# Feed-forward entry of a four-layer block: last probability transposes inside attending, sums of x before variances, later transposes of x

## What is computed

```
x = x + tanh(g_xattn[0]) * xattn0(layernorm(x), ctx, ctx)        # one head, 154 keys
x = x + tanh(g_ffn[0])   * ffn0(layernorm(x))                    # 8 experts, every token
x = x + tanh(g_xattn[1]) * xattn1(layernorm(x), ctx, mask)       # 8 heads of 64
x = x + tanh(g_ffn[1])   * ffn1(layernorm(x))                    # routed to one of 8 experts

ffn0: for each expert: acc += (silu(x @ Wg) * (x @ Wu)) @ Wd     # 256 -> 1024 -> 256
```

## Time and profile before

| what | value |
|---|---|
| runs | 1256.52, 1256.78 and 1260.38 us, median 1256.78 |
| the profiled execution's own time | 1260.54 us, of which the span from first to last instruction is 1258.8 us |
| PE busy | 1232.6 us (98% of the span) |
| DVE busy | 1054.3 us (84%) |
| ACT busy | 729.2 us (58%) |
| POOL busy | 880.5 us (70%) |
| mean granted clock | 0.995 |

### The profile page before, as it was taken

One profiled execution on the slowest core, in us unless ns is written; L12 is line 12 of the kernel. 1 busy time (PEld: TensorE's weight loads), 2 busy tenths in 40 slices (PEclk: granted clock), 3 DMA queues, 4 the chain that ended last, 5 costly groups with the idle time before them and its releaser, 6 DMA issues.

```text
span 1258.8 us, 18431 instructions
## 1 busy us (share of the span) xinstructions
PE 1232.6 (98%) x6152; PEld 995.4 (79%) x6152; DVE 1054.3 (84%) x1775; ACT 729.2 (58%) x1509; POOL 880.5 (70%) x833
## 2 busy tenths in 40 slices
PE   7999999999999999999999999999999999999998
PEld 5778888888888888888888888888888887787775
DVE  5887889898899999999999999888999974667546
ACT  2455566656666666666666666666566545545543
POOL 3735688888887888888877888888888626443435
PEclk9999999999999999999999999999999999999999
DMA  4020200000110000000000000000100330000131
GB/s 137 26 92 1 94 26 26 26 26 26 41 36 26 26 26 26 26 26 26 26 26 26 26 26 26 26 26 31 42 29 1 117 118 1 18 26 10 35 98 63
DMA packets 42366, 48.28 MB, mean 38 GB/s; under 512 B 4239, under 2 KB 40143, under 8 KB 42015
## 3 DMA queue, kind: packets, MB, share of 16 engines
q1 hardware_dynamic: 38720, 43.07, 10.4%
q0 software_dynamic: 1440, 3.41, 0.8%
q10 hardware_dynamic: 2111, 0.63, 0.2%
HBM read 37.36 MB, written 10.29 MB: 38 GB/s over the span
## 4 chain that ended last, share of the span: by engine, by line
PE 91%; DVE 4%; ACT 3%; issue 1%; DMA 0%; POOLq 0%; ACTq 0%; POOL 0%; DVEq 0%
PE bank L1307 25%; PE bank L1308 25%; PE bank L1309 25%; ACT PC L1050 2%; PE bank L1545 2%; PE bank L1554 1%; PE bank L1269 1%; PE bank L1707 1%; PE bank L1724 1%; PE bank L1251 1%; DVE nmC L2101 1%; PE bank L1529 1%; PE bank L1213 1%; PE bank L1657 1%; PE bank L1479 1%
## 5 line engine op out<-in xcount | busy, mean ns | idle before, releaser
L1307 PE MATMUL bank<-xop_hi,w_hi 128*128 128x512 f32 x896 | 351.9, 393 | 1.7 <-ACT half_g L948 1.2
L1308 PE MATMUL bank<-xop_lo,w_hi 128*128 128x512 f32 x896 | 352.4, 393 | 0.0
L1309 PE MATMUL bank<-xop_hi,w_lo 128*128 128x512 f32 x896 | 351.4, 392 | 0.0
L1958 DVE TENSOR_TENSOR hid_lo<-hid,hid_hi 128x512 fp32r<-128x512 f32 x228 | 220.2, 979 | 14.1 <-ACT hid_hi L972 9.8
L1307 PEld LDWEIGHTS bank<-xop_hi,w_hi 128*128 128x128 f32 x896 | 168.9, 188 | 42.4 <-ACT half_g L948 1.5
L1308 PEld LDWEIGHTS bank<-xop_lo,w_hi 128*128 128x128 f32 x896 | 168.6, 188 | 38.2
L1309 PEld LDWEIGHTS bank<-xop_hi,w_lo 128*128 128x128 f32 x896 | 168.6, 188 | 37.7
L972 ACT CAST hid_hi<-hid 128x512 fp32r<-128x512 f32 x228 | 140.8, 622 | 57.9 <-DVE hid L1950 57.9
L956 ACT ACTIVATE s<-bank 128x512 f32<-128x512 f32 x128 | 78.3, 612 | 102.5 <-PE bank L1309 102.5
L1307 PE MATMUL bank<-hid_hi,wd_hi 128*128 128x512 f32 x344 | 136.2, 396 | 0.6 <-DVE hid_lo L1958 0.6
L1308 PE MATMUL bank<-hid_lo,wd_hi 128*128 128x512 f32 x344 | 136.2, 396 | 0.0
(11 more groups left out here) (273 smaller groups left out, 2615.1 us busy)
## 6 DMA issues: line engine op xcount, KB each, us to landing
raw_gu<-in_L_ffn_Wg_dram SPq DMA_DIRECT2D x32, 256.0 KB, 2.7
raw_gu<-in_L_ffn_Wu_dram SPq DMA_DIRECT2D x32, 256.0 KB, 3.1
raw_d<-in_L_ffn_Wd_dram SPq DMA_DIRECT2D x32, 256.0 KB, 3.7
slots<-empty_row SPq DMA_DIRECT2D x1, 2080.0 KB, 11.1
xr<-slots SPq DMA_DIRECT2D x8, 260.0 KB, 4.5
x_res<-in_x_dram SPq DMA_DIRECT2D x4, 512.0 KB, 5.3
x_mid<-x_res SPq DMA_DIRECT2D x1, 2048.0 KB, 9.2
x_res<-x_mid SPq DMA_DIRECT2D x4, 512.0 KB, 5.4
```

Of the source, the lines that this page charges most:

```text
L1307: mm(ps, w, a, start=start, stop=False, skip_group_check=True)
L1308: mm(ps, w, a_low, start=False, stop=False, skip_group_check=True)
L1309: return mm(ps, w_low, a, start=False, stop=True, skip_group_check=True)
L1958: nc.vector.tensor_tensor(out=hid_lo[n % 2][h][:], in0=hid[h][:], in1=hid_hi[n % 2][h][:].bitcast(F32), op=ALU.subtract).then_inc(lo_ready ...
```

## The change

Nothing is added or removed but a few waits; the instructions are the same and stand in another order.

- PE: for chunk 2 the attending is cut in two halves, and the probability transposes of chunk 3 stand between them instead of behind both. ACT copies these before it takes the first two high parts of x.
- DVE: the sums T2 and T3 stand before `a_add_half(2, 1)`, T4 right behind it, the first two low parts before `ln2_variances(2)`; `ln2_normed(2)` comes two low parts later, `a_add(3)` two low parts later again. `ln2_variances(3)` moves from before group 0 to behind its second sum, `ln2_normed(3)` from behind the first sum to behind `hid_sum` of block 22.
- PE: the transposes of chunk 2 move from before `product7(0, "g")` to before `product7(0, "u")`; those of chunk 3 from inside group 0 (before `down_step(-1, 5)`, that is behind `product4(0, "g")`) into group 1, behind `product1(1, "u")`.
- ACT: `x_raw_out(2)` moves behind the first silu of group 0, `x_raw_out(3)` into group 1 behind `fork(1, "u")`, and the high parts of blocks 22 and 12 of group 0 behind `fork(1, "g")`.

```diff
             x_raw_out(0)
             a_exps(NC - 1)
             x_raw_out(1)
+            a_pT_out(NC - 1)
             x_hi_first(0)
-            a_pT_out(NC - 1)
...
             for n in range(GROUPS + 1):
                 fork(n, "g")
+                if n == 1:
+                    hi_part(0, "22")
+                    hi_part(0, "12")
                 hi_part(n - 1, "11")
                 fork(n, "u")
-                if n == 0:
-                    x_raw_out(2)
+                if n == 1:
+                    x_raw_out(3)
...
                 silu_psum(n, "11", s11, bank[SUM_BANK["g"]], p2_ps)
+                if n == 0:
+                    x_raw_out(2)
                 t_hi_part(n - 1, "T4")
                 keep_u2(n, "u")
...
                 silu_psum(n, "21", s21, bank[FORK_BANK["g"]], p4_ps)
-                if n == 0:
-                    x_raw_out(3)
                 if n == 1:
                     x_hi_rest(1)
-                hi_part(n, "22")
-                hi_part(n, "12")
+                if n > 0:
+                    hi_part(n, "22")
+                    hi_part(n, "12")
...
-            def a_attend(u):
+            def a_attend(u, of=range(CT)):
                 pe.wait_ge(a_pT, 2 * u + 2)
-                for j in range(CT):
+                for j in of:
...
-                a_p_transposes(u)
+                if u < NC - 1:
+                    a_p_transposes(u)
...
-                a_attend(u)
+                if u == NC - 2:
+                    a_attend(u, range(2))
+                    a_p_transposes(NC - 1)
+                    a_attend(u, range(2, CT))
+                else:
+                    a_attend(u)
...
                 product1(n, "u")
+                if n == 1:
+                    x2_transposes(NC - 1)
...
                 down_step(n - 1, 1)
-                if n == 0:
-                    x2_transposes(NC - 2)
                 product7(n, "g")
...
                 product3(n, "u")
+                if n == 0:
+                    x2_transposes(NC - 2)
                 product7(n, "u")
...
                 product4(n, "g")
-                if n == 0:
-                    x2_transposes(NC - 1)
...
             x_first_sum(nc.vector, dve, 0)
+            dve.wait_ge(x_raw_ready, 4)
+            dve.wait_ge(x_sum_ready[0], 1)
+            x_sum(nc.vector, 0, X_T2, X_22, X_T1)
+            x_sum(nc.vector, 0, X_T3, X_22, X_T3)
             a_add_half(2, 1)
-            ln2_variances(2)
-            x_other_sums(nc.vector, dve, 0)
+            dve.wait_ge(x_sum_ready[0], 2)
+            x_sum(nc.vector, 0, X_T4, X_21, X_T2)
             for i in range(2):
                 x_lo_out(nc.vector, dve, 0, i)
-            ln2_normed(2)
+            ln2_variances(2)
             for i in range(2, 4):
                 x_lo_out(nc.vector, dve, 0, i)
+            ln2_normed(2)
+            for i in range(4, 6):
+                x_lo_out(nc.vector, dve, 0, i)
             a_add(3)
-            for i in range(4, 7):
-                x_lo_out(nc.vector, dve, 0, i)
-            ln2_variances(3)
+            x_lo_out(nc.vector, dve, 0, 6)
...
             def group(n):
                 sum_22(n, "g")
-                if n == 0:
-                    ln2_normed(3)
                 sum_12(n, "g")
                 if n == 0:
+                    ln2_variances(3)
                     sum_22(n, "u")
...
                 hid_sum(n, "22", half22, sum22)
+                if n == 0:
+                    ln2_normed(3)
                 hid_sum(n, "12", half12, sum12)
```

## The result

| | median, us | runs | lowest, highest |
|---|---|---|---|
| before | 1256.80 | 20 | 1256.07, 1260.38 |
| changed | 1259.15 | 20 | 1256.68, 1262.63 |

The ratio on record is 1.0016, 95% interval 1.0008 to 1.0023. It is computed over all the runs and is not quite the quotient of the two medians, which differ by 2.35 us (1.0019). The change made the kernel slower, but by less than the 0.3% that I had set as the bound for a change, and on the other side of no change than I had forecast. The comparison was finer than I had allowed for: with 20 runs of each the interval reaches about 1 us to either side.

The account below looks back on a forecast made before the run. PE, busy 98%, was taken as the bound; +0.25 - 1.07 - 3.42 - 0.44 + 0.5 + 0.8 = -3.4 gave 1257.1 us from the profiled execution, beside 1256.2 from the median; forecast 1256.5, range 1253.4 to 1259.9.

Parts of the forecast that it names:

- the halved stretch: Clock at 1.2 GHz from 61.79 to 68.62 us in the profile of before; none expected in the changed kernel, -3.42 us.
- PE finds them ready: -1.07: Last attending, chunk 3: PE no longer waits for ACT's copied probabilities at 59.30, a gain of 1.07 us.
- T2 and T3 at 0.63 each: DVE's sums ahead of the second add of chunk 2: the add ends at 59.7, at most 60.5; no PE wait.
- Rival D: Wait for probabilities becomes one for the add of chunk 2; PE loses 0.2 to 0.5 us; no separate chance given.
- The fork wait, -0.44: fork(1, "g"), before the first down product, no longer stands behind two high parts: its 0.44 us wait goes.
- the further "1.1 us": Fork wait at 82.74, reckoned longer in runs without the halved stretch: up to 1.1 us more gain against the median.
- keep_u2's 1.22: PE's wait behind the transposes of chunk 2 moves from side g to side u, not removed: 0 us.
- +0.5 for sum_22: At product4(0, "u"), PE wants DVE's sum_22(0, "u") at 73.75 but it ends at 74.3: 0.5 us lost.
- +0.8 for the down product's banks: First down product waits for ACT's copies of chunk 3, ending at 80.8: a new wait of 0.8 us.
- Rival B: The median of before holds the halved stretch too, so 3.4 us comes off it: 1253.4 us; chance 0.13.
- Rival A: New PE waits near 71 to 80 us drop the clock in the changed kernel too: 1259.9 us; chance 0.11.
- Rival C: Lower-clock stretch near 1055 us, second attention, comes or goes, some 1.7 us: 1254.8 or 1258.2; chance 0.12.

Follow-up runs that it names:

- pt_only: Kernel before with only the probability transposes of chunk 3 between the halves of attending chunk 2 and ACT's copy of them earlier; median 1260.55 against 1257.48 us, ratio 1.0014.
- b_again: The kernel before, run again unchanged; median 1257.09 against 1257.48 us, ratio 0.9995.
- a_keep: Changed kernel with ACT's copies of chunk 2 of x behind keep_u2 of side u instead of ahead; median 1257.90 against 1256.75 us for before, ratio 1.0011.
- b_delay: Kernel before with 5 idle matmuls (1.15 us) right ahead of the first down product; median 1259.22 against 1256.68 us, ratio 1.0016.
- a_again: The changed kernel, run again unchanged; median 1259.30 against 1256.68 us for the kernel before, ratio 1.0021.
- b_keep: Kernel before with ACT's copies of chunk 2 of x behind keep_u2 of side g; median 1256.64 against 1256.75 us, ratio 0.9998.
- b_x3: Kernel before with copies of chunk 2 of x behind keep_u2 of side g and transposes of chunk 3 behind product4(0, "u"); median 1259.64 against 1256.68 us, ratio 1.0021.
- later_only: Kernel before with only the change's later part: ACT's, PE's and DVE's lists from the low parts on; median 1258.97 against 1257.48 us, ratio 1.0014.

## Why the prediction was wrong

I forecast 1256.5, a little faster and within no change; the median was 1259.15, slower. The first down product came at 82.71, behind the 82 that I had named as a sign that the reading is wrong. Counted from the transposes of chunk 1 (52.84 in my list), the second add ends at 8.25 instead of 7.26, half_u's sum at 22.65 instead of 21.46 and the down product starts at 29.09 instead of 27.96; the kernel before without the halved stretch, which I had at 27.98 (31.40 - 3.42), measured 27.91. So my list of the changed kernel was 1.0 us short at the second add, and from half_u's sum on it was right (6.44 against 6.5).

- **The step that failed is "PE finds them ready: -1.07", counted as gain, with DVE's sums and low parts at nothing.** I took PE's idle time as gain because PE is 98% busy. Up to `product4(0, "u")` DVE was the bound; only 0.4 us of the 1.07 lay ahead of its first low part even with nothing else changed, and the sum that this product waits for ended only 0.18 earlier (22.65 against 22.83). pt_only shows the gain turn into a wait of 1.80. My own sum of DVE's list gave "cover of 0.2 to 1 us", and I costed what lies under that cover at nothing.
- **T2 and T3 at 0.63 each** (0.68 in length; 0.63 is from start to start). They took 0.91 and 1.75, and the add ended 0.82 too late for PE: this is the 1.0 us at the add. My upper end, T1's 1.10 for each, was no upper end: T1 had lain beside POOL for part of its length. Rival D, this same mechanism, was priced at 0.2 to 0.5.
- **The transposes of chunk 3** I had "start unhindered" in group 1, at no cost, since PE's work stayed the same. They left a place where PE had to wait for DVE anyway and cost 0.80 us in the new one.
- **Attending in pieces** I costed as free. From start to start without the waits it takes 7.15 us in the changed kernel (1.89, 3.61 and 1.65) and 6.82 in b_again (3.45 and 3.37): +0.33, of which 0.10 comes back in the step of the probability transposes (0.94 against 1.04).
- **The fork wait, -0.44, and the further "1.1 us"** against the median: nothing. An execution of before without the halved stretch has no such wait.
- **keep_u2's 1.22 moved, not removed**: right (74.50). And a_keep shows that removing it would have been worth nothing in the passage (29.10).
- **+0.5 for sum_22 and +0.8 for the down product's banks**: right in place, 0.17 and 0.41 in size.
- **The halved stretch**: that the median lacked it was right (b_again; 14 of the 20 runs of before lie below 1257.3). It was halved for 61.57 to 68.40 us, 0.2 ahead of my window. Rival B fell. Rival A did not come: the clock in both profiles of the changed kernel is 1.00 from 55 to 84 us.
- **Rival C** is the second half of the result. I gave it 0.12 and saw it as luck of both signs; in b_delay, as in the changed kernel, it falls on one side in nearly every run (none of 11 and none of 32 at 1.000; 3 of the 32 at 0.999). Its price, 2.35 less the passage's 1.2, is about 1.2 us.

Together, counted another way: waits of PE in the passage of a_again are 0.15, 0.81, 0.30, 1.22 and 0.43, in all 2.91, against 2.29 in b_again: +0.62. With +0.23 for the pieces that is 0.85 of the 1.20; the rest I put down to the first matmul behind each wait (0.47 to 0.50 us instead of 0.39) and did not measure apart. Then 1.2 us of clock, of which b_delay shows that a delay brings it, and no run shows why.

No version beat the kernel before: b_keep, at 0.9998 with an interval from 0.9988 to 1.0008, is equal to it.

## What to carry to other kernels

Before a wait of the busiest engine is counted as gain, add up what the next engine has to deliver behind it: with an engine that has had no gap for 10 us, PE's wait only moves to its next result. A wait removed by putting work ahead of an instruction that feeds that chain costs what it puts there. Work of PE that stands in front of such a result is free as long as PE is early for it; moved behind the result, it costs its full length. And where the clock has several outcomes, look at how a plain delay of the same size moves the median, before a difference of two microseconds is put down to the order of instructions.

## What I had not expected of the hardware

- With 1.15 us of added matmuls at 81 us the median came out 2.54 us higher (interval 0.9 to 3.1) and no run kept a mean clock of 1.000; the halved stretch of the profile is 970 us later.
- Halved stretches had lengths of 3.41 or 6.83 us. From the first down product on, one of 3.41 costs 0.6 to 1.2 us against b_keep's 1173.34 and b_x3's 1173.47, the one of 6.83 at 1177.7 in pt_only 2.5 (1175.88), two of 6.83 in later_only 5.2 (1178.55).
- A 128x512 sum on DVE took 0.68 us alone and 0.91, 1.10 and 1.75 beside POOL's weight splitting, while POOL's 128x512 one went from 1.26 to 1.59.
